# Query projections by seven block products for 18 cross heads, in a fused four-layer kernel on one Trainium2 core

## The chip, the core and the metric

The kernel runs on one core of a Trainium2 chip. The metric is the device time of one execution in microseconds (us). The profile is one execution taken by the hardware profiler. Engines are named PE (TensorE), DVE (VectorE), ACT (ScalarE), POOL (GpSimd) and SP (SyncE, which issues the loads here).

## The reference, cut to what matters

Four layers run one after the other on a stream x of 8 x 128 tokens of width 256, all against the same context of 8 x 128 tokens. Layers 0 and 1 are attention layers with 16 heads of size 16 and an MLP each; layer 3 has a self-attention, a cross-attention and an MLP. Layer 2, in which the change lies, has two cross-attentions with 16 heads of size 128, then an MLP:

```python
def _cross_attention(q_in, kv_in, wq, bq, wk, bk, wv, bv, wo, bo, bias_k, bias_v):
    qh = (q_in @ wq + bq).reshape(b, q_len, H, K)
    kh = (kv_in @ wk + bk).reshape(b, t, H, K)
    vh = (kv_in @ wv + bv).reshape(b, t, H, K)
    kh = jnp.concatenate([kh, jnp.broadcast_to(bias_k, (b, 1, H, K))], axis=1)
    vh = jnp.concatenate([vh, jnp.broadcast_to(bias_v, (b, 1, H, K))], axis=1)
    scale = jnp.sqrt(jnp.asarray(K, q_in.dtype))
    logits = jnp.einsum('bqhk,bthk->bhqt', qh, kh) / scale
    weights = jax.nn.softmax(logits, axis=-1)
    ctx = jnp.einsum('bhqt,bthk->bqhk', weights, vh).reshape(b, q_len, H * K)
    return ctx @ wo + bo
```

H is 16, K is 128. q_in is the normalised stream, kv_in the context.

## The kernel before, in words

All tensors are float32. A product that needs accuracy is made in three passes: each operand is cut into an upper part (rounded to fp32r, "hi") and a lower part (the rest, "lo"), and PE makes hi x hi, hi x lo and lo x hi (`PASSES`). POOL cuts the weights: a cast writes hi, a subtraction writes lo.

**Stages.** Layers 0 and 1 run first and layer 2's MLP and layer 3 last, each by an order written out by hand for every engine (`ORDER_ONE`, `ORDER_TWO`). Between them stand the two cross-attentions of layer 2. They run in 16 turns (`TURNS`): attention j = 1, 2 and turn = 0 to 7, two heads a turn. Below, (j,turn) is a turn. Every engine has its own program, a loop over the turns at the end of `tensor_program`, `vector_program`, `scalar_program` and `gpsimd_program`; each executes its instructions in order, and semaphores tie them together. SP issues the loads in the loop of `sync_program`.

**PE in a turn (L1014 on):** scores of both heads (L960); output projections of the turn before (L994, four pieces); keys of the next turn (L928 or L914); values (L946, four pieces); transposes of the softmax weights (L970); queries of the next turn (L914); weighing of the values (L981). Results go to the eight banks of PSUM. `claim` makes PE wait until the bank's last content has been drained. The keys of the next turn take the banks in which the scores of this turn stand, so they wait for DVE's `bshifted` (L1301); the queries of the next turn take the banks of the values.

**Seven products.** For the keys of (1,3) to (1,7) and (2,1) to (2,7) the 256 x 256 weights of two heads are taken as a matrix of 2 x 2 blocks and the context as 2 x 2 blocks, and their product is made with seven block products instead of eight (`SEVEN`, `seven_products` L920): 21 matmuls of 512 columns instead of 24. POOL makes the sums of the weight blocks, the forms S1 to S4, and cuts them (`cut_forms` L1860, eight operations). The sums of context blocks, the halves T1 to T4, are made once: `begin_halves` on POOL in (1,0) (L1886, six operations), `make_halves` on DVE in (1,1) (L1332, four operations in a chain), upper parts by ACT at the end of (1,1) (L1691), `lower_halves` on POOL after that (L1896, four operations). ACT copies the first product out of its bank (`copy_product` L1633), and DVE adds the others onto it in seven operations (`add_products` L1304, `end_products` L1320). Three of the products take a bank a second time: the fifth waits for ACT's copy, the sixth for DVE's first sum (L1310), the seventh for its second (L1313).

**DVE in a turn (L1423 on):** maximum and shift of both heads' scores (L1296, L1301); output additions (L1379); sum and reciprocal (L1347, L1351); between them the key sums; value drains (L1360); query drains with scale and bias (`queries_of` L1281, which the profile shows as L1072, two per turn); lower parts of the weighed values (L1367).

**ACT in a turn (L1671 on):** exponentials (L1644, L1647); key drains or the product's copy (L1635); copies of the transposed weights (L1655); upper parts of the weighed values (L1485).

**POOL in a turn (L1964 on):** query weights of the next turn (L1846, L1848), value weights of this turn, then the two divides (L1929), each of which waits for DVE's reciprocal; then the keys' forms of the turn after next, the output weights, and in some turns weights of later layers: `cut_up` (L1739, L1741) for M2 and L3c in (2,1) to (2,4), `cut_weights` (L1724, L1726) from (2,5) on. At the end of (1,7) POOL also adds the output bias to x (L2002, four operations).

**Loads.** The weights of the last stage are loaded into `weights` in four pieces in (1,1) to (1,4) (`EARLY`) and three pieces after the last key products (`LATE`), whose places hold the forms and halves until then.

Of the kernel before, what the change touches and what calls it, by code (L numbers as in the profile page):

```python
# [8 lines left out]
F32R = mybir.dt.float32r  # L9
# [43 lines left out]
EARLY = [(0, AT_C["L2_w_fc2"]), (AT_C["L3_w_qkv"], AT_C["L3_w_q"]), (AT_C["L3_w_q"], AT_C["L3_w_co"]), (AT_C["L3_w1"], AT_C["L3_w2"])]  # L53
# [43 lines left out]
def in_seven(j, turn):  # L97

    return turn > 0 and (j, turn) >= (1, 3)
# [6 lines left out]
SEVEN = (("A11", "B11", 0, "product_copied", "P1"), ("S2", "T2", 1, "products_added", "U2"), ("S3", "T3", 2, "products_added", "U3"),  # L106
         ("S1", "T1", 3, "products_added", "C22"), ("A22", "T4", 0, "products_added", "C21"), ("S4", "B22", 1, "products_added", "C12"),
         ("A12", "B21", 2, "products_added", "C11"))
# [41 lines left out]
class Signal:  # L150
# [16 lines left out]
    "w_c_loaded", "w_fc2_loaded", "w_late_loaded", "masks_loaded", "bv_loaded", "wq_loaded0", "wq_loaded1", "wk_loaded0", "wk_loaded1", "wv_loaded", "wo_loaded",  # L167
# [10 lines left out]
    "product_made", "product_copied", "products_added", "form_made", "forms_hi", "forms_lo", "half_made", "half_ended", "halves_hi", "halves_lo",  # L178
# [76 lines left out]
class Memory:  # L255
    def block(self, name, part):
        if name in RAW_BLOCKS:
            return self.k_cut[part][:, RAW_BLOCKS[name], :]
        return self.forms[part][:, MADE_BLOCKS[name], :]

    def half_of(self, name, part):
        if name in HALVES:
            c, n = HALVES[name]
            return self.bcT[part][:, c, n * BANK:(n + 1) * BANK]
        return self.halves[part][:, MADE_HALVES[name], :]

    def __init__(self, nc, ctx):
# [80 lines left out]
        with ExitStack() as b:  # L348
# [7 lines left out]
            self.cut = {n: parts(n, [P, 2, HK]) for n in ("q0", "q1")}  # L356
            self.k_cut = parts("k", [P, 4, HK])
            for n in range(2):
                self.cut[f"k{n}"] = [part[:, 2 * n:2 * n + 2, :] for part in self.k_cut]
# [9 lines left out]
            s2("room", [P, 5600])  # L369
            forms_hi = s2("forms hi", [P, 4, HK], F32R)  # L370
        of_halves, of_forms = (slice(*at) for at in (LATE[1], LATE[2]))
# [293 lines left out]
def tensor_program(nc, m, s, d):  # L665
# [60 lines left out]
    def once(signal, value):  # L726

        if signal not in loaded:
            loaded.add(signal)
            pe.wait_ge(s[signal].sem, value)  # L730
# [1462 lines left out]
```

## Time and profile before

| what | us |
|---|---|
| median of 3 runs | 1036.88 (1036.3 to 1036.94) |
| the profiled execution, its own time | 1035.47 |
| its span, first to last instruction | 1034.2 |
| PE busy | 1000.6 (97%) |
| DVE busy | 767.9 (74%) |
| POOL busy | 651.7 (63%) |
| ACT busy | 577.0 (56%) |

The granted clock of PE is 1.0 of full speed over the whole span. Matmuls overlap, so the time between the starts of two phases says what a phase costs PE, and the durations of single matmuls do not. In a timeline each line has the start, the duration, the engine, the source line, the operation, what it writes and reads, and in brackets the idle time before it with what ended it; a duration after which xN stands covers N instructions.

### The profile page before, as it was taken

What the parts mean: (1) busy time and instruction counts of PE and PEld (TensorE: products, weight loads), DVE (VectorE), ACT (ScalarE), POOL (GpSimd) and SP (SyncE); (2) the same over time, 40 slices, a digit from 0 to 9 for tenths busy, and PEclk for the clock granted to TensorE, in tenths of its full rate; (3) what the DMA queues carried; (4) which work ended last, traced back from release to release, by engine and by line L of the source; (5) the groups of instructions that cost most, each with busy time, mean ns of one, the idle gap of its engine ahead of it and who ended that gap; (6) DMA issues with size and microseconds to landing.
All of it is one profiled execution on the core that took longest, in us unless ns stands there. A gap on an engine that the chain in (4) does not pass through costs nothing.

```text
span 1034.2 us, 21141 instructions
## 1 busy us (share of the span) xinstructions
PE 1000.6 (97%) x8239; PEld 900.8 (87%) x8239; DVE 767.9 (74%) x1229; ACT 577.0 (56%) x1288; POOL 651.7 (63%) x595
## 2 busy tenths in 40 slices
PE   7899999999999999999998999999998999989998
PEld 7788888888899999999997999999998988777877
DVE  7997888998257677876767867777865387898761
ACT  5998888797534422223233332222226489999982
POOL 6885476755578574434367666755534388999960
PEclk9999999999999999999999999999999999999999
DMA  8200001000121220121120111110120000000000
GB/s 329 119 2 2 1 2 42 2 1 2 47 77 42 72 82 28 56 82 42 41 85 21 42 42 42 34 38 12 31 103 1 1 2 1 2 2 2 12 11 21
DMA packets 33931, 40.73 MB, mean 39 GB/s; under 512 B 2127, under 2 KB 31273, under 8 KB 32297
## 3 DMA queue, kind: packets, MB, share of 16 engines
q1 hardware_dynamic: 33833, 39.38, 11.4%
q8 instruction: 67, 1.10, 0.4%
q14 instruction: 31, 0.25, 0.1%
HBM read 38.32 MB, written 1.05 MB: 38 GB/s over the span
## 4 chain that ended last, share of the span: by engine, by line
PE 81%; POOL 9%; DVE 4%; ACT 4%; issue 1%; DMA 0%; SPq 0%; DVEq 0%; ACTq 0%; POOLq 0%
PE psum L914 11%; PE psum L793 9%; PE psum L809 9%; PE psum L946 8%; PE psum L994 8%; PE psum L981 6%; PE psum L928 5%; PE psum L960 5%; PE psum L835 5%; POOL C tile L1792 3%; PE psum L720 3%; PE psum L970 3%; PE psum L825 3%; PE psum L850 2%; POOL C tile L1798 2%; PE psum L864 1%
## 5 line engine op out<-in xcount | busy, mean ns | idle before, releaser
L1929 POOL TENSOR_TENSOR B tile<-B tile,B rec 128x1024 f32<-128x1024 f32 x32 | 61.0, 1909 | 161.6 <-DVE B rec L1351 161.6
L1798 POOL TENSOR_TENSOR A tile<-A tile,outer rec 128x1024 f32<-128x1024 f32 x48 | 91.0, 1905 | 57.9 <-DVE outer rec L1190 57.8
L1655 ACT COPY B PT<-psum 128x512 f32<-128x512 f32 x64 | 32.9, 601 | 139.0 <-PE psum L970 139.0
L1072 DVE TENSOR_SCALAR B qT<-psum,cols 128x1024 f32<-128x1024 f32 (+1 forms) x38 | 44.0, 1166 | 71.6 <-PE psum L914 70.2
L1570 ACT ACTIVATE A tile<-A tile,outer min 128x128 f32<-128x128 f32 (+1 forms) x256 | 92.2, 448 | 2.6 <-DVE outer min L1183 2.5
L1570 ACT ACTIVATE C tile<-C tile,outer min 128x128 f32<-128x128 f32 x256 | 77.9, 399 | 0.5 <-DVE outer min L1183 0.4
L946 PE MATMUL psum<-B v hi,cT hi 128*128 128x256 f32 x256 | 72.1, 282 | 0.3 <-ACT B kT L1485 0.3
L946 PE MATMUL psum<-B v hi,cT lo 128*128 128x256 f32 x256 | 71.8, 281 | 0.0
L946 PE MATMUL psum<-B v lo,cT hi 128*128 128x256 f32 x256 | 71.8, 281 | 0.0
L1798 POOL TENSOR_TENSOR C tile<-C tile,outer rec 128x1024 f32<-128x1024 f32 x32 | 60.5, 1895 | 6.0 <-DVE outer rec L1190 6.0
L1176 DVE TENSOR_TENSOR A tile<-m,psum 128x1024 f32<-128x1024 f32 x48 | 56.5, 1216 | 9.2 <-PE psum L825 8.0
L1188 DVE TENSOR_REDUCE outer sum<-A tile 128x4 f32<-128x1024 f32 (+1 forms) x48 | 58.0, 1208 | 4.9 <-ACT A tile L1570 4.9
L1536 ACT COPY A PT<-psum 128x512 f32<-128x512 f32 x96 | 51.4, 591 | 18.3 <-PE psum L835 10.9
L1485 ACT ACTIVATE B OT0 hi<-psum,cols 128x512 fp32r<-128x512 f32 x32 | 21.9, 688 | 70.9 <-PE psum L981 70.8
L981 PEld LDWEIGHTS psum<-B PT,B v 128*128 128x128 f32 x512 | 59.4, 192 | 1.0
L960 PE MATMUL psum<-B kT,B qT 128*128 128x128 f32 x512 | 59.8, 275 | 0.0
L981 PE MATMUL psum<-B PT,B v 128*128 128x128 f32 x512 | 59.7, 275 | 0.0
L960 PEld LDWEIGHTS psum<-B kT,B qT 128*128 128x128 f32 x512 | 58.5, 192 | 0.1
L809 PE MATMUL psum<-weights,C aT 128*128 128x256 f32 x256 | 57.2, 380 | 1.2 <-ACT C aT L1527 1.2
L809 PE MATMUL psum<-weights,A aT 128*128 128x256 f32 x256 | 57.8, 380 | 0.1
L835 PEld LDWEIGHTS psum<-ident,A tile 128*128 128x128 f32 x384 | 42.1, 141 | 18.2 <-issue 11.4
L1183 DVE TENSOR_REDUCE outer min<-A tile 128x4 f32<-128x1024 f32 (+1 forms) x48 | 55.9, 1207 | 0.0
(327 smaller groups left out, 3470.5 us busy)
## 6 DMA issues: line engine op xcount, KB each, us to landing
weights<-in_weights_c SPq DMA_DIRECT2D x5, 1024.0 KB, 6.3
raw<-in_wq SPq DMA_DIRECT2D x32, 128.0 KB, 2.7
raw<-in_wk SPq DMA_DIRECT2D x32, 128.0 KB, 3.0
raw<-in_wv SPq DMA_DIRECT2D x16, 256.0 KB, 2.8
raw<-in_wo SPq DMA_DIRECT2D x16, 256.0 KB, 2.7
weights<-in_weights_a SPq DMA_DIRECT2D x1, 3072.0 KB, 21.6
weights<-in_weights_a SPq DMA_DIRECT2D x1, 2048.0 KB, 12.4
wide<-in_bias_v SPq DMA_DIRECT2D x2, 1024.0 KB, 10.3
```

The costliest lines, as they stand in the source:

```text
L793: i = pe.matmul(bank(z)[:, n * T:(n + 1) * T], w[wp][:, c, n * P:(n + 1) * P], h[hp][:, c, :], start=(c, wp, hp) == (0, 0, 0), stop=c == C ...
L809: i = pe.matmul(bank(z)[:, 0:D], part.aT(k)[:, c, b * P:(b + 1) * P], w2[:, c, :], start=c == 0, stop=c == FC - 1)
L835: i = pe.transpose(bank(4 + half)[:, j * P:(j + 1) * P], part.tiles[u % 4][:, q * P:(q + 1) * P], m.ident[:, :])
L914: i = pe.matmul(bank(z + n), wt[wp][:, c, :], src[sp][:, c, n * BANK:(n + 1) * BANK], start=(c, wp, sp) == (0, 0, 0), stop=c == C - 1 and ...
L946: i = pe.matmul(bank(z)[:, k * 2 * HK:(k + 1) * 2 * HK], m.bcT[cp][:, c, (2 * n + k) * S:(2 * n + k + 1) * S], m.cut["v"][wp][:, c, :], st ...
L960: i = pe.matmul(bank(z + b // 4)[:, (b % 4) * S:(b % 4 + 1) * S], m.qT[h][:, b * S:(b + 1) * S], m.kT[h][:, b * S:(b + 1) * S], start=True ...
L981: i = pe.matmul(bank(z)[:, k * P:(k + 1) * P], m.vv[:, 4 * n + k, h * HK:(h + 1) * HK], m.bPT[:, h, n, k * P:(k + 1) * P], start=True, sto ...
L994: i = pe.matmul(bank(z)[:, k * D:(k + 1) * D], m.bOT[h][op][:, (2 * n + k) * S:(2 * n + k + 1) * S], m.cut["o"][wp][:, h, :], start=(h, op ...
L1188: dve.tensor_reduce(part.sum[:, u % 4, 0:ly.per], tile(u, ly.nk), AX.X, ALU.add).then_inc(s["sum_made"].sem, s["sum_made"].mark((st, u)))
L1570: i = act.activation(of_head, of_head, ACT.Exp, bias=part.min[:, u % 4, h:h + 1], scale=-1.0)
L1798: pool.tensor_tensor(tile(u, ly.nk), tile(u, ly.nk), part.rec[:, u % 4, 0:ly.per].unsqueeze(2).to_broadcast([P, ly.per, ly.nk]), ALU.mult) ...
L1929: pool.tensor_tensor(tv, tv, m.brec[:, h, :].unsqueeze(2).to_broadcast([P, B, S]), ALU.mult).then_inc(s["normalised"].sem, s["normalised"] ...
```

## The change

- The queries of 18 heads, those of (1,4) to (1,7) and (2,3) to (2,7), come from seven block products too, with their own semaphores, blocks, forms and halves. DVE adds them after the value drains, ACT copies the first after the transposed weights, POOL makes the forms in place of the plain cut. The query and key functions become one, with a `kind`.
- The queries' halves are sums of blocks of the stream and are made for each attention: for j = 1 DVE begins them at the end of (1,1) and ends them at the end of (1,2), ACT makes the upper parts and POOL the lower ones at the end of (1,2); for j = 2 POOL begins them at the end of (2,0), DVE ends them at the end of (2,1), ACT makes the upper parts there, and POOL the lower ones in (2,2), after the divides and before the key forms.
- `make_halves` becomes `end_halves` and moves on DVE from the middle of (1,1) to its end, behind `weigh_heads`.
- In (2,0) ACT copies the first key product between the two exponentials, not after them.
- POOL adds the output bias in (2,0), after the output weights' cut, not at the end of (1,7).
- The four cuts of L3c's up-weights move on POOL from (2,1) to (2,4) to the end of (2,7). Their weights, L3's first output weights and L3c's query weights (1.5 MB in three pieces) are loaded after the last query products.
- The factor 1/sqrt(128) moves from the query drain and two column scalings to the exponential.

```diff
-EARLY = [(0, AT_C["L2_w_fc2"]), (AT_C["L3_w_qkv"], AT_C["L3_w_q"]), (AT_C["L3_w_q"], AT_C["L3_w_co"]), (AT_C["L3_w1"], AT_C["L3_w2"])]
+LATER = [(AT_C["L3_w1"], AT_C["L3_w2"]), (AT_C["L3_w_ao"], AT_C["L3_w_q"]), (AT_C["L3_w_q"], AT_C["L3_w_kv"])]
+EARLY = [(0, AT_C["L2_w_fc2"]), (AT_C["L3_w_qkv"], AT_C["L3_w_ao"]), (AT_C["L3_w_kv"], AT_C["L3_w_co"])]
...
-def in_seven(j, turn):
-
-    return turn > 0 and (j, turn) >= (1, 3)
+FIRST_SEVEN = {("k", 1): 3, ("k", 2): 1, ("q", 1): 4, ("q", 2): 3}
+
+
+def in_seven(kind, j, turn):
+
+    return turn >= FIRST_SEVEN[kind, j]
...
     def project_pair(j, kind, turn):
-        if kind == "k" and in_seven(j, turn):
-            seven_products(j, turn)
+        if in_seven(kind, j, turn):
+            seven_products(j, kind, turn)
             return
...
-        affine(m.qT[head % 2][:, :], m.psum[:, z:z + 2, :].rearrange("p a b -> p (a b)"), SCALEK, m.col[f"L2_bq{j}"][:, head:head + 1]).then_inc(
+        affine(m.qT[head % 2][:, :], m.psum[:, z:z + 2, :].rearrange("p a b -> p (a b)"), None, m.col[f"L2_bq{j}"][:, head:head + 1]).then_inc(
...
+    def begin_halves(j, kind):
+        made, raw = s[kind + "_half_begun"], m.halves_raw[kind]
+        for name, of, (less, more), spare in (("T1", 0, ("B11", "B12"), 2), ("T3", 2, ("B12", "B22"), 3)):
+            if name == "T3":
+                dve.wait_ge(made.sem, made.at((j, "T1")))
+            dve.tensor_tensor(raw[:, of, :], m.half_of(kind, more, 0), m.half_of(kind, less, 0), ALU.subtract)
+            dve.tensor_tensor(raw[:, spare, :], m.half_of(kind, more, 1), m.half_of(kind, less, 1), ALU.subtract).then_inc(made.sem, made.mark((j, "lo", name)))
+            dve.wait_ge(made.sem, made.at((j, "lo", name)))
+            dve.tensor_tensor(raw[:, of, :], raw[:, of, :], raw[:, spare, :], ALU.add).then_inc(made.sem, made.mark((j, name)))
...
+        shared = {kind: not last and in_seven(kind, j, turn + 1) for kind in "kq"}
+        if shared["k"]:
+            add_products(j, "k", turn + 1)
         divide_by_sum(j, turn, 1)
-        if shared:
-            end_products(j, turn + 1)
-        if (j, turn) == (1, 1):
-            make_halves()
+        if shared["k"]:
+            end_products(j, "k", turn + 1)
         for n in range(4) if turn else ():
             values_of(j, turn, n)
-        if not last:
+        if shared["q"]:
+            add_products(j, "q", turn + 1)
+            end_products(j, "q", turn + 1)
+        elif not last:
             queries_of(j, 2 * turn + 2)
             queries_of(j, 2 * turn + 3)
         for h in range(2):
             weigh_heads(j, turn, h)
+        if (j, turn) == (1, 1):
+            end_halves(1, "k")
+            begin_halves(1, "q")
+        if (j, turn) in ((1, 2), (2, 1)):
+            end_halves(j, "q")
...
-        for h in range(2):
-            exponentials(j, turn, h)
-        if not last and in_seven(j, turn + 1):
-            copy_product(j, turn + 1)
-        elif not last:
+        exponentials(j, turn, 0)
+        if (j, turn) == (2, 0):
+            copy_product(2, "k", 1)
+        exponentials(j, turn, 1)
+        if turn and not last and in_seven("k", j, turn + 1):
+            copy_product(j, "k", turn + 1)
+        elif not last and not in_seven("k", j, turn + 1):
             keys_of(j, 2 * turn + 2)
             keys_of(j, 2 * turn + 3)
         for h in range(2):
             turn_weights(j, turn, h)
+        if not last and in_seven("q", j, turn + 1):
+            copy_product(j, "q", turn + 1)
...
+        if (j, turn) == (2, 2):
+            lower_halves(2, "q")
         if turn < NP_ - 2:
             cut_pair(j, "k", turn + 2)
         elif (j, turn) == (1, NP_ - 2):
             cut_pair(2, "k", 0)
         cut_output(j, turn)
         if (j, turn) == (1, 0):
-            begin_halves()
+            begin_halves(1, "k")
         if (j, turn) == (1, 1):
-            lower_halves()
+            lower_halves(1, "k")
+        if (j, turn) == (1, 2):
+            lower_halves(1, "q")
+        if (j, turn) == (2, 0):
+            bias_x()
+            begin_halves(2, "q")
         if (j, turn) == (1, NP_ - 1):
             cut_pair(2, "q", 0)
         if j == 2 and 1 <= turn < 5:
             cut_up("M2", turn - 1)
-            cut_up("L3c", turn - 1)
...
+        if (j, turn) == (2, NP_ - 1):
+            for n in range(4):
+                cut_up("L3c", n)
...
+    sp.wait_ge(s["q_product_made"].sem, s["q_product_made"].at((2, NP_ - 1, "A12")))
+    for at in LATER:
+        load_last("w_later_loaded", *at)
```

## Rows read from the trace of the kernel before

**Rows 1.** The page: busy time, the chain that ended last, one costly group
```profile
PE 1000.6 (97%) x8239; PEld 900.8 (87%) x8239; DVE 767.9 (74%) x1229; ACT 577.0 (56%) x1288; POOL 651.7 (63%) x595
...
PE 81%; POOL 9%; DVE 4%; ACT 4%; issue 1%; DMA 0%; SPq 0%; DVEq 0%; ACTq 0%; POOLq 0%
...
L1929 POOL TENSOR_TENSOR B tile<-B tile,B rec 128x1024 f32<-128x1024 f32 x32 | 61.0, 1909 | 161.6 <-DVE B rec L1351 161.6
```

**Rows 2.** Timeline of PE in (1,2): keys, sixth product, values, queries, weighing
```profile
365.50 0.40 PE L928 MATMUL psum<-cT hi,B k hi 128*128 128x512 f32 x1
...
368.95 0.40 PE L928 MATMUL psum<-cT hi,B forms hi 128*128 128x512 f32 x1
...
370.32 0.28 PE L946 MATMUL psum<-B v hi,cT hi 128*128 128x256 f32 x1
...
377.64 0.47 PE L914 MATMUL psum<-B hT hi,B q1 hi 128*128 128x512 f32 x1
...
383.21 3.73 PE L981 MATMUL psum<-B PT,B v 128*128 128x128 f32 x32
```

**Rows 3.** Timeline of DVE from the end of (1,1) through (1,2)
```profile
356.20 1.65 DVE L1367 SCALAR_TENSOR_TENSOR B OT1 lo<-psum,cols,B OT1 hi 128x512 fp32r<-128x512 f32 x2
358.17 1.22 DVE L1296 TENSOR_REDUCE B max<-psum 128x8 f32<-128x1024 f32 x1 [0.32 <-PE psum L960]
...
367.16 0.69 DVE L1310 TENSOR_TENSOR B kT<-psum,B kT 128x512 f32<-128x512 f32 x1 [0.40 <-PE psum L928]
...
380.69 1.28 DVE L1072 TENSOR_SCALAR B qT<-psum,cols 128x1024 f32<-128x1024 f32 x1 [3.82 <-PE psum L914]
```

**Rows 4.** Timeline of POOL: divide and key forms in (1,2); one cut in (2,1)
```profile
371.55 1.90 POOL L1929 TENSOR_TENSOR B tile<-B tile,B rec 128x1024 f32<-128x1024 f32 x1 [2.76 <-DVE B rec L1351]
373.41 0.46 POOL L1870 TENSOR_TENSOR weights<-raw 128x128 f32<-128x128 f32 x1
...
378.42 0.61 POOL L1846 CAST B o hi<-raw 128x512 fp32r<-128x512 f32 x1
...
603.33 0.61 POOL L1739 CAST C w1 hi<-weights 128x512 fp32r<-128x512 f32 x1
...
605.25 0.39 POOL L1846 CAST B q1 hi<-raw 128x256 fp32r<-128x256 f32 x1
```

**Rows 5.** Timelines of DVE, POOL and PE in (2,0) and (2,1)
```profile
564.06 0.69 DVE L1310 TENSOR_TENSOR B kT<-psum,B kT 128x512 f32<-128x512 f32 x1 [0.56 <-ACT B kT L1635]
...
575.98 1.29 POOL L1848 TENSOR_TENSOR B o lo<-raw,B o hi 128x512 fp32r<-128x512 f32 x1
...
591.36 0.28 PE L946 MATMUL psum<-B v hi,cT hi 128*128 128x256 f32 x1
```

**Rows 6.** Timelines of DVE and POOL in (1,1): halves, and POOL's work beside
```profile
336.77 0.64 DVE L1335 TENSOR_TENSOR weights<-cT hi,weights 128x512 f32<-128x512 f32 x1
337.45 2.27 DVE L1337 TENSOR_TENSOR weights<-weights,cT lo 128x512 f32<-128x512 f32 x1
...
336.94 2.23 POOL L1929 TENSOR_TENSOR B tile<-B tile,B rec 128x1024 f32<-128x1024 f32 x1 [0.64 <-DVE B rec L1351]
...
357.65 5.01 POOL L1899 TENSOR_TENSOR weights lo<-weights,weights lo 128x512 fp32r<-128x512 f32 x4 [9.91 <-ACT weights lo L1691]
```

**Rows 7.** Timeline of POOL at the end of (1,0): begun halves, then cuts
```profile
321.43 1.27 POOL L1891 TENSOR_TENSOR weights<-cT hi 128x512 f32<-128x512 f32 x1
...
329.17 0.40 POOL L1846 CAST B q1 hi<-raw 128x256 fp32r<-128x256 f32 x1
...
331.49 0.61 POOL L1846 CAST B v hi<-raw 128x512 fp32r<-128x512 f32 x1
```

**Rows 8.** Timeline of POOL at the end of (2,7), and a DMA group
```profile
777.31 1.29 POOL L1726 TENSOR_TENSOR weights lo<-weights,C qkv hi 128x512 fp32r<-128x512 f32 x1
778.54 1.93 POOL L2006 MEMSET C vaug<- 128x512 f32 x4
788.05 0.70 POOL L1713 TENSOR_TENSOR outer rstd<-outer ve,half 128x2 f32<-128x2 f32 x1 [7.59 <-DVE outer ve L1113]
...
weights<-in_weights_c SPq DMA_DIRECT2D x5, 1024.0 KB, 6.3
```

More of the change, by code:

```diff
@@ L355, in __init__ @@
             self.kT = [s2(f"kT{k}", [P, B * S]) for k in range(2)]
[L356 to L359, printed above, removed]
+            self.cut, self.blocks = {}, {}
+            for kind in "qk":
+                self.blocks[kind] = parts(kind, [P, 4, HK])
+                for n in range(2):
+                    self.cut[f"{kind}{n}"] = [part[:, 2 * n:2 * n + 2, :] for part in self.blocks[kind]]
             self.cut["v"] = parts("v", [P, 2, 2 * HK])
@@ L1688, in scalar_program @@
         if (j, turn) == (1, 1):
-            act.wait_ge(s["half_ended"].sem, s["half_ended"].at("T4"))
-            for n in range(4):
-                act.copy(m.halves[0][:, n, :], m.halves_raw[:, n, :]).then_inc(s["halves_hi"].sem, s["halves_hi"].mark(n))
+            upper_halves(1, "k")
+        if (j, turn) in ((1, 2), (2, 1)):
+            upper_halves(j, "q")
         if last and j == 1:
@@ L1858, in cut_head, with bias_x, cut_forms @@
         cut(j, f"{kind}{k}", head, (f"w{kind}_loaded{k}", 16 * ((j - 1) * NP_ + head // 2 + 1)))
-    def cut_forms(j, turn):
-        made, raw, forms, event = s["form_made"], m.k_raw, m.forms_raw, (j, turn)
+    def bias_x():
+        for k in range(NS):
+            pool.wait_ge(s["nxn_made"].sem, s["nxn_made"].at((k, SB - 1)))
+            pool.tensor_tensor(m.x(k), m.x(k), m.row("L2_bo2").unsqueeze(1).to_broadcast([P, SB, D]), ALU.add).then_inc(
+                s["x_biased"].sem, s["x_biased"].mark(k))
+    def cut_forms(j, kind, turn):
+        made, upper, lower = s[kind + "_form_made"], s[kind + "_forms_hi"], s[kind + "_forms_lo"]
+        raw, forms, blocks, event = m.blocks_raw[kind], m.forms_raw[kind], m.blocks[kind], (j, turn)
         a21, a22, a11, a12 = (raw[:, n, :] for n in range(4))
@@ L1888, in begin_halves @@
+        pool.tensor_tensor(m.forms[kind][1][:, :, :], forms[:, :, :], m.forms[kind][0][:, :, :], ALU.subtract).then_inc(
+            lower.sem, lower.mark((*event, "made")))
+    def begin_halves(j, kind):
+        made, raw = s[kind + "_half_made"], m.halves_raw[kind]
         for name, of, (less, more), spare in (("T1", 0, ("B11", "B12"), 2), ("T3", 2, ("B12", "B22"), 3)):
             if name == "T3":
-                pool.wait_ge(made.sem, made.at("T1"))
-            pool.tensor_tensor(raw[:, of, :], m.half_of(more, 0), m.half_of(less, 0), ALU.subtract)
@@ L1892, in begin_halves @@
[L1892 to L1896 removed]
+                pool.wait_ge(made.sem, made.at((j, "T1")))
+            pool.tensor_tensor(raw[:, of, :], m.half_of(kind, more, 0), m.half_of(kind, less, 0), ALU.subtract)
@@ L1897, in lower_halves @@
+            pool.tensor_tensor(raw[:, spare, :], m.half_of(kind, more, 1), m.half_of(kind, less, 1), ALU.subtract).then_inc(made.sem, made.mark((j, "lo", name)))
+            pool.wait_ge(made.sem, made.at((j, "lo", name)))
+            pool.tensor_tensor(raw[:, of, :], raw[:, of, :], raw[:, spare, :], ALU.add).then_inc(made.sem, made.mark((j, name)))
+    def lower_halves(j, kind):
+        hi, lo = s[kind + "_halves_hi"], s[kind + "_halves_lo"]
         for n in range(4):
-            pool.wait_ge(s["halves_hi"].sem, s["halves_hi"].at(n))
@@ L1991, in gpsimd_program @@
             cut_weights("L3c", "kv"[turn - 5])
+        if (j, turn) == (2, NP_ - 1):
+            for n in range(4):
+                cut_up("L3c", n)
         if last and j == 1:
```

190 lines of the change are left out of this document (96 added, 94 removed).

## The prediction

> **What bounds the kernel now.** I read the page first, then the timeline of each engine over one turn. The page [rows 1] has TensorE (PE) busy for 97% of the span and carrying 81% of the chain that ended last. GpSimd (POOL) idles 161.6 us ahead of its 32 divides, 5 us each. So the idle time of the others is worth nothing by itself; what counts is where PE waits for them.
>
> In turn (1,2) (attention 1, turn 2; I write (j,turn) throughout) PE starts the key products at 365.50, the values at 370.32, the queries at 377.64 and the weighing at 383.21 [rows 2], one behind the other. VectorE (DVE) has room in the second half of a turn, 3.82 us ahead of the first query drain, and almost none in the first: from the maximum at 358.17 to the first key sum at 367.16 it waits 0.40 us [rows 3]. These slacks can be read off, and the change spends them in a few places.
>
> **Query products.** Plain queries take PE 383.21 - 377.64 = 5.57 us a turn (24 matmuls), seven products 370.32 - 365.50 = 4.82 us (21) [rows 2]. Nine turns take the new form, (1,4) to (1,7) and (2,3) to (2,7): 9 x 0.75 = **6.7 us** gained.
>
> For each of them DVE makes seven sums of some 0.7 us in place of two drains of 1.28 us [rows 3]. The last should end, as in the keys, within 2 us of the last product. PE weighs for 3.73 us [rows 2] before the scores want it, and DVE's own next work starts about then. I cost the sums at nothing; their cover is DVE's idle 3.82 us, and ACT (ScalarE) makes its copy when it waits for the weighing. Without cover each turn gives back its 0.75.
>
> POOL's cut of the queries grows from four operations, 2.3 us, to the eight of the keys, 378.42 - 373.41 = 5.0 us [rows 4]. The 2.7 more lie ahead of a divide, where POOL idles; nothing is due there.
>
> **The key copy, turn (2,0).** DVE's first key sum waits 0.56 us for ACT's copy [rows 5]. With the copy ahead of the second exponential that wait goes, and DVE, busy until then, is the next that is late. The bias additions leave the place before the forms, so PE has those earlier, but its sixth product wants the same sum. Gain: **0.6 us** for both edits.
>
> **DVE at the end of (1,1): ten subtractions before the next maximum.** Before, DVE made the key halves in mid-turn, where it had room. Now four operations that end the key halves and six that begin the query halves stand between the last output part, which ends at 356.20 + 1.65 = 357.85, and the maximum at 358.17 [rows 3]. A start follows the last by 0.7 us [rows 6]. Four end at 360.7, ten at 364.9: a lag of 6.7 us.
>
> They also meet POOL. The second of the four took 2.27 us beside a POOL multiplication that took 2.23 [rows 6] where it takes 1.90 alone [rows 4]. Now POOL makes its four lower halves, 5.01 us, 1.25 each [rows 6], from about 361.5, while DVE is at its fifth to tenth. I let them take turns, which adds 4 x 1.25 less 0.3 of overlap: DVE ends at 369.6, a lag of 11.4.
>
> The Trainium skill, "SBUF — State Buffer", section "SBUF: two separate sides", says that a DVE operation with two SBUF inputs and a GpSimd one that reads SBUF lock each other out for the whole instruction. The trace agrees where it shows the case (2.27 us beside 2.23); by this rule the sum is the one below, without it that of the first rival.
>
> What PE feels: its key products claim the score banks and wait for DVE. The first sum ended at 367.16 + 0.69 = 367.85 after waiting 0.40 for PE [rows 3]; the product that takes its bank starts at 368.95 [rows 2]. So 1.5 us of lag are free. PE loses 11.4 - 1.5 = **9.9 us** in (1,2), 5.2 if nothing meets at the port. Outputs aside, everything behind on PE's queue is later by the same.
>
> **End of (1,2), felt in (1,3).** Four subtractions, 2.8 us, of which DVE had 0.3 idle, with POOL waiting for them: lag 2.5, loss 1.0. Then POOL has the four lower halves (5.0, from 0.65 us after DVE's maximum starts), the new query cut 5.0 and the value cut 1.9 (the same two operations as in 605.25 - 603.33 [rows 4]), and ends 12.5 us after that maximum. PE wants the values 370.32 - 358.17 = 12.15 us after an undelayed one [rows 2, 3], here 12.15 - 2.5 + 1.0 = 10.65. It waits 1.9. Together **2.9 us**.
>
> **POOL at the end of (2,0), felt in (2,1).** The output cut ends at 577.3 [rows 5], less the 0.6 gained. Then come four bias additions of 1.25, the six begun halves in 329.17 - 321.43 = 7.7, the query cuts in 331.49 - 329.17 = 2.3 [rows 7] and the value cut, 1.9: 576.7 + 16.9 = 593.6. PE wants the values at 591.36 [rows 5], now 590.8. It waits **2.8 us**. The DMA wait that now stands before the query cut vanishes in this.
>
> **End of (2,1), felt in (2,2).** Four subtractions, lag 2.5 alone. POOL, late from the step before, is in its query forms and value cut, so I add 2.5 for blocked starts: lag 5.0, loss 3.5 (1.0 at the low end). Next, the lower halves stand after the divides: the second divide ends 371.55 + 1.90 - 358.17 = 15.3 us after the maximum [rows 3, 4], and 5.0 more is 20.3. The query products would start 19.5 us after an undelayed maximum [rows 2, 3], 18.0 after this one. PE waits 2.3. Together **5.8 us**.
>
> **The tail.** The four cuts of the last up-weights leave (2,1) to (2,4), where POOL idled, for the end of (2,7): 4 x 1.92 = 7.7 us after 777.31 + 1.29 = 778.6, then 1.9 of memsets, ending at 788.2. The first root of the last stage ran at 788.05 after an idle 7.59 [rows 8]: **0.2 us**. Three loads (1.5 MB) are issued later, after the last query products, most of a turn before POOL wants them; 1 MB lands in 6.3 us [rows 8], and on SP's queue only two other late loads stand behind. Two tiny scalings go near the start: nothing.
>
> **The sum.** Lost: 9.9 + 2.9 + 2.8 + 5.8 + 0.2 = 21.6. Gained: 6.7 + 0.6 = 7.3. Net +14.3 us. The profiled execution took 1035.47 us (span 1034.2, 1.3 outside it), 1.4 under the median of 1036.88. Against its own time the sum gives 1049.8; against the median, which is what will be measured, **1051.2**. A measurement of this kernel can tell about 0.2% (2.1 us) from no change.
>
> **Rivals.**
> - *No clash at the port.* DVE ends its ten at 364.9 and PE loses 5.2 there, 3.3 in (2,2). Net 5.2 + 2.9 + 2.8 + 3.3 + 0.2 - 7.3 = +7.1: 1044.0. For it: one overlap in the trace is thin evidence, and DVE's many operations on PSUM run beside POOL unharmed. Against: [rows 6] is the very operation. Chance 0.15.
> - *The lags never reach PE.* The place is the key products of (1,2). If the slack there and before the value cuts is larger than I read, only the saving is left: 1036.9 - 7.3 = 1029.6, faster. It decides when all losses together stay under 7.3, which (1,2) alone exceeds unless it costs a fraction of my figure. For it: POOL's idle time is large on the whole. Against: PE's queue runs in order and its claims are written out. Chance 0.10; another 0.03 that losses and gains cancel, at about 1037.
> - *The query products give nothing.* DVE's sums or POOL's forms hold PE up in each of the nine turns: 1051.2 + 6.7 = 1057.9. Against: the keys do the same without it. Chance 0.07.
>
> **How the numbers follow.** The forecast has 0.65, with its own range 1047 to 1055: 9.9 and 5.8 can each be 2 too much, and blocked starts can add 3. For 8 in 10 the range reaches down past the first rival to 1041. Faster 0.10, same 0.03, slower 0.87.
>
> **What would show it.** In the changed kernel's trace: query products of 4.8 us in nine turns; the maximum of (1,2) some 11 us after the last output part, with DVE subtractions of 1.3 to 2 us in between; PE idle for several us in and before the key products of (1,2); waits of PE for POOL's value cut in (1,3) and (2,1), and for the lower halves before the queries of (2,2). I am wrong if PE has under 7 us of waits between (1,1) and (2,3), or if those ten subtractions take 0.7 us each.

## The result, and the profile after

The changed kernel takes **1050.99 us**, median of 4 runs (1049.48 to 1052.34), against 1036.59 for the kernel before beside it (4 runs, 1035.2 to 1036.94): a ratio of 1.0142, with a 95% interval of 1.0129 to 1.0155. It is 14 us slower; 1051.2 was forecast. The profiled execution took 1049.48 us, its span 1048.3.

The page of the kernel after, to be read against [rows 1]:

```profile
PE 1004.6 (96%) x8212; PEld 900.8 (86%) x8212; DVE 799.6 (76%) x1286; ACT 586.3 (56%) x1305; POOL 697.4 (67%) x645
...
PEclk9999999999999989999999999999999999999999
...
PE 71%; POOL 13%; DVE 8%; ACT 4%; issue 3%; DMA 0%; SPq 0%; DVEq 0%; POOLq 0%; ACTq 0%
...
L1983 POOL TENSOR_TENSOR B tile<-B tile,B rec 128x1024 f32<-128x1024 f32 x32 | 60.7, 1900 | 116.5 <-DVE B rec L1379 116.5
```

PE's share of the chain fell from 81% to 71%; POOL and DVE took it. POOL's idle time ahead of the divides fell from 161.6 to 116.5 us, as it has 45.7 us more work. One slice of the granted clock shows 8, where before there was none. 27 matmul instructions fewer (three in each of nine turns) say that the query products are there.

What PE waited for in the attentions, longest first (the view of waits, PE, 300 to 800 us of the kernel after; columns: engine, what the instruction writes and its line, the releaser; us in total, times, longest):

```profile
PE psum L946 <- DVE B tile L1319: 5.5, 1, 5.5
PE psum L946 <- DVE B kT L1328: 4.4, 4, 1.7
PE psum L964 <- POOL B v lo L1895: 3.1, 2, 1.9
PE psum L946 <- POOL weights lo L1953: 1.8, 1, 1.8
```

Before, the longest single wait in this stretch was one of 1.5 us, for ACT's copy in (2,0), and none of these four rows was there. The first row is the key products of (1,2) waiting for DVE's shift, the second the sixth key product waiting for DVE's first sum, in (1,2), (1,3), (2,0) and (2,2), the third the values of (1,3) and (2,1) waiting for POOL's value cut, the last the queries of (2,2) waiting for the lower halves.

DVE at the end of (1,1), which answers to [rows 3] (timeline of the kernel after):

```profile
357.17 0.68 DVE L1363 TENSOR_TENSOR weights<-cT hi,weights 128x512 f32<-128x512 f32 x1
...
360.55 0.69 DVE L1356 TENSOR_TENSOR weights<-B hT lo 128x512 f32<-128x512 f32 x1
361.27 1.67 DVE L1358 TENSOR_TENSOR weights<-weights 128x512 f32<-128x512 f32 x1
362.98 1.67 DVE L1355 TENSOR_TENSOR weights<-B hT hi 128x512 f32<-128x512 f32 x1
364.57 1.76 DVE L1356 TENSOR_TENSOR weights<-B hT lo 128x512 f32<-128x512 f32 x1
366.36 1.63 DVE L1358 TENSOR_TENSOR weights<-weights 128x512 f32<-128x512 f32 x1
367.92 1.21 DVE L1314 TENSOR_REDUCE B max<-psum 128x8 f32<-128x1024 f32 x1
```

And POOL and PE behind it (timelines, the same kernel):

```profile
360.77 6.68 POOL L1953 TENSOR_TENSOR weights lo<-weights,weights lo 128x512 fp32r<-128x512 f32 x4 [14.30 <-ACT weights lo L1676]
...
370.53 0.77 PE L946 MATMUL psum<-cT hi,B k hi 128*128 128x512 f32 x1 [5.47 <-DVE B tile L1319]
371.10 0.63 PE L946 MATMUL psum<-cT lo,B k hi 128*128 128x512 f32 x1
...
377.16 0.50 PE L946 MATMUL psum<-cT hi,B k forms hi 128*128 128x512 f32 x1 [0.30 <-DVE B kT L1328]
...
378.75 0.28 PE L964 MATMUL psum<-B v hi,cT hi 128*128 128x256 f32 x1
```

Ten operations stand between the output parts and the maximum. Six take 0.68 to 0.69 us. The last four take 1.63 to 1.76, and they are the ones beside POOL's four lower halves, which take 6.68 us together against the 5.01 of [rows 6]. The maximum is 10.35 us later than its normal place (357.57, 1.97 behind the start of the last output part, as in [rows 3]); this delay of DVE's maximum is called the lag below. PE reaches the key products and stops for 5.47 us.

The same comparison for whole turns, from the start of one turn's scores to the next (read off PE's timeline). "Plain" is the length with no wait:

| turn | before | after | what is in it |
|---|---|---|---|
| (1,2) | 30.60 | 39.41 | + 8.8, DVE's lag |
| (1,3) | 30.60 | 32.98 | - 0.6 query products, + 0.8 keys, + 2.2 value cut |
| (1,4) to (1,6), (2,3) to (2,6) | 30.60 | 29.99 | - 0.61 each |
| (2,0) | 21.96 | 22.85 | - 0.7 for the copy, + 1.6 low clock |
| (2,1) | 30.60 | 31.93 | + 1.3, value cut |
| (2,2) | 30.60 | 34.46 | - 0.6, + 2.7 keys, + 1.8 lower halves |

The gains are 9 x 0.61 = 5.5 and 0.7; the losses 8.8, 3.0 and, over (2,0) to (2,2), 1.6 + 1.3 + 4.5 = 7.4. That is 13.0 more at the end of the attentions. The stage began 0.6 us earlier in this execution (324.29 against 324.89; in other kernels of this study it began anywhere from 324.3 to 327.4), and 1.6 came later, nearly all of it behind 900 us. 13.0 - 0.6 + 1.6 = 14.0, the difference of the two executions (1049.48 - 1035.47).

Two of these items were in no step of the prediction: a lower clock in (2,0), and one behind 900 us. The granted clock by stretches of the kernel after (windows of PE: stretch; its length, busy time and instructions; granted clock; DMA share; GB/s):

```profile
360.00:365.00 5.00, 5.00 (x43) 1.00 0.00 0
365.00:370.00 5.00, 0.06 (x1) 0.94 0.00 0
370.00:376.00 6.00, 5.47 (x13) 0.50 0.16 48
376.00:380.00 4.00, 3.69 (x20) 0.97 0.00 0
572.00:574.00 2.00, 1.13 (x4) 1.00 0.00 0
574.00:578.00 4.00, 4.00 (x12) 0.57 0.00 0
578.00:580.00 2.00, 2.00 (x11) 1.00 0.00 0
```

In (1,2) that is hidden, since DVE is late with its first key sum anyway (377.16 waits 0.30 for it): in e5_plain below the same stretch is half as long, 370.17 to 373.59, PE then waits 1.57 us for that sum, and (1,2) is 39.41 us all the same. In (2,0) nothing hides it.

### The profile page after: what moved, and what is told of

It reads as the page before. It is cut to its first block, busy times and chain, and to the rows that moved or that the text cites. A ratio compares the mean times of both kernels' runs of the same rounds, so it can differ in the third digit from the quotient of the medians.

```text
span 1048.3 us, 21233 instructions
## 1 busy us (share of the span) xinstructions
PE 1004.6 (96%) x8212; PEld 900.8 (86%) x8212; DVE 799.6 (76%) x1286; ACT 586.3 (56%) x1305; POOL 697.4 (67%) x645
## 4 chain that ended last, share of the span: by engine, by line
PE 71%; POOL 13%; DVE 8%; ACT 4%; issue 3%; DMA 0%; SPq 0%; DVEq 0%; POOLq 0%; ACTq 0%
PE psum L810 9%; PE psum L826 9%; PE psum L946 8%; PE psum L964 7%; PE psum L931 5%; PE psum L1012 5%; PE psum L852 5%; PE psum L999 5%; PE psum L978 4%; PE psum L738 3%; PE psum L842 3%; PE psum L867 3%; POOL C tile L1839 2%; PE psum L988 2%; PE psum L881 2%
## 5 line engine op out<-in xcount | busy, mean ns | idle before, releaser
L1983 POOL TENSOR_TENSOR B tile<-B tile,B rec 128x1024 f32<-128x1024 f32 x32 | 60.7, 1900 | 116.5 <-DVE B rec L1379 116.5
L852 PEld LDWEIGHTS psum<-ident,A tile 128*128 128x128 f32 x384 | 42.1, 141 | 18.2 <-issue 11.4
L1388 DVE TENSOR_TENSOR B v<-psum,B bv 128x512 f32<-128x512 f32 x64 | 42.1, 684 | 18.4 <-PE psum L964 17.5
```

Of the source, the lines that this page charges most:

```text
L852: i = pe.transpose(bank(4 + half)[:, j * P:(j + 1) * P], part.tiles[u % 4][:, q * P:(q + 1) * P], m.ident[:, :])
L1983: pool.tensor_tensor(tv, tv, m.brec[:, h, :].unsqueeze(2).to_broadcast([P, B, S]), ALU.mult).then_inc(s["normalised"].sem, s["normalised"] ...
```

## The experiments

The theory at this point: the loss is waits of PE at five places, each caused by what the change puts on DVE or POOL ahead of something PE wants, and the query products themselves gain. The rivals: DVE's ten operations are not what counts, but POOL's lower halves; the long DVE operations come from something other than POOL; the query products gain nothing. Below, "changed" is the changed kernel.

**e1_order.** In (1,1) the halves of the queries first:

```diff
         if (j, turn) == (1, 1):
-            end_halves(1, "k")
             begin_halves(1, "q")
+            end_halves(1, "k")
```

> The changed kernel with one swap on DVE at the end of (1,1): the six operations that begin the query halves come before the four that end the key halves, so POOL, which waits for the latter, is idle during all ten. Theory (a port that DVE and POOL lock against each other): all ten take 0.7 us, the maximum of (1,2) starts 7 us after the last output part instead of 10.7, and PE's key products are now held by POOL's lower key halves, which end some 13 us after it; PE's loss in (1,2) falls from 9.0 to 5 to 7 us, the time to 1047 to 1049. Rival (the operations are slow by themselves, because of their operands): four of them still take 1.6 to 1.8 us and the time stays at 1051.

Measured: 1049.44 us, ratio 1.0147 [1.0119, 1.0175], no different from the changed kernel. DVE and then POOL and PE (timelines of e1_order):

```profile
357.94 0.68 DVE L1355 TENSOR_TENSOR weights<-B hT hi 128x512 f32<-128x512 f32 x1
...
364.09 0.69 DVE L1369 TENSOR_TENSOR weights<-weights,cT lo 128x512 f32<-128x512 f32 x1
364.70 1.21 DVE L1314 TENSOR_REDUCE B max<-psum 128x8 f32<-128x1024 f32 x1
```

```profile
365.51 4.95 POOL L1953 TENSOR_TENSOR weights lo<-weights,weights lo 128x512 fp32r<-128x512 f32 x4 [18.29 <-ACT weights lo L1676]
...
370.72 0.77 PE L946 MATMUL psum<-cT hi,B k hi 128*128 128x512 f32 x1 [4.89 <-POOL weights lo L1953]
```

With POOL's lower halves behind them, all ten operations take 0.7 us and DVE's lag is 6.4 instead of 10.35. PE still starts its keys at 370.72, because now it waits for the lower halves. So the clash is real, and undoing it alone saves only what the next late thing leaves: (1,2) fell from 39.41 to 36.91, 2.5 us. It was lost again further on: (1,3) is 34.64 instead of 32.98, where the granted clock is low from 411.3 to 414.7, and (2,0) and (2,1) together are 56.43 instead of 54.79, where the low stretch stands behind the wait for the value cut (602.4 to 605.9) and no longer in (2,0).

**e2_ten_mid.** The ten operations where DVE has room, in mid-turn:

```diff
+        if (j, turn) == (1, 1):
+            end_halves(1, "k")
         for n in range(4) if turn else ():
             values_of(j, turn, n)
+        if (j, turn) == (1, 1):
+            begin_halves(1, "q")
...
-        if (j, turn) == (1, 1):
-            end_halves(1, "k")
-            begin_halves(1, "q")
```

> The changed kernel with all ten halves operations of (1,1) in mid-turn: the four ahead of the value drains, as before the change, the six behind them. Theory (DVE's lag ahead of the maximum is what PE feels in (1,2)): the maximum of (1,2) is on time, PE starts the key products without a wait, the 9.0 us lost there go, 1042. Rival (half of that loss is PE's lowered clock or POOL's lower halves): 1044 to 1047.

Measured: 1043.04 us, ratio 1.0078 [1.0053, 1.0104], 8.0 under the changed kernel by the medians; by the two ratios, each to the kernel before timed beside it, 6.6. In the traces (1,2) is 30.60 us, to the hundredth what it was before, 8.8 less than in the changed kernel; the other turns of the table keep their losses and are 1.1 longer together ((1,3) 33.19, (2,1) 32.14, (2,2) 35.14, with a low clock from 626.9 to 630.3). In mid-turn two of the ten are held up as well, and it costs nothing (timeline of e2_ten_mid):

```profile
336.84 2.27 DVE L1365 TENSOR_TENSOR weights<-weights,cT lo 128x512 f32<-128x512 f32 x1
...
346.24 1.78 DVE L1356 TENSOR_TENSOR weights<-B hT lo 128x512 f32<-128x512 f32 x1
...
357.56 1.23 DVE L1314 TENSOR_REDUCE B max<-psum 128x8 f32<-128x1024 f32 x1 [0.32 <-PE psum L978]
```

The maximum has its 0.32 us of idle back, as in [rows 3]. The place of the ten operations is the whole loss of (1,2), 8.8 us.

**e3_ends_mid.** The four operations that end the query halves, in (1,2) and (2,1), likewise ahead of the query drains:

```diff
+        if (j, turn) in ((1, 2), (2, 1)):
+            end_halves(j, "q")
         if shared["q"]:
             add_products(j, "q", turn + 1)
             end_products(j, "q", turn + 1)
...
-        if (j, turn) in ((1, 2), (2, 1)):
-            end_halves(j, "q")
```

> The changed kernel with the four operations that end the query halves ahead of the query drains in (1,2) and (2,1) rather than behind the output parts. Theory: the key products of (1,3) and (2,2) are on time (2.6 to 3.6 us back), POOL gets the upper halves 3 us earlier, so most of the wait for the value cut in (1,3) goes and the wait for the lower halves in (2,2) shrinks from 2.0 to about 1: some 6 us less, 1045. Rival (POOL's own work sets these two turns, not DVE's lag): 2 us less or nothing, 1049 to 1051.

Measured: 1043.11 us, ratio 1.0077 [1.006, 1.0093]. (1,3) is 29.98, so both of its waits are gone, that for DVE's sum and that for the value cut. The prediction priced the two apart, yet one place of four operations makes both. POOL shows why (timelines, first of the changed kernel, then of e3_ends_mid):

```profile
400.16 5.06 POOL L1953 TENSOR_TENSOR weights lo<-weights,B q halves hi 128x512 fp32r<-128x512 f32 x4 [10.50 <-ACT B q halves hi L1676]
```

```profile
397.03 5.02 POOL L1953 TENSOR_TENSOR weights lo<-weights,B q halves hi 128x512 fp32r<-128x512 f32 x4 [5.25 <-ACT B q halves hi L1676]
```

POOL had been idle for 10.5 us, waiting for ACT, and ACT for DVE's four operations. Made earlier, they let POOL begin 3.7 us sooner (1.5 us behind the start of the scores of (1,3), at 395.56, in place of 5.2 behind it, at 394.99), and its value cut is in time. (2,2) is 31.01: what is left above 29.99 is 1.0 of lower halves (PE waits 0.78 for them there). (2,0) fell from 22.85 to 21.23, since the clock stayed at 1.00 there, and (2,1) rose from 31.93 to 35.20: PE, that much earlier, waits 2.9 us for the value cut and then has its low clock there, 601.5 to 604.9.

**e4_bias_back.** The bias additions again at the end of (1,7):

```diff
         if (j, turn) == (2, 0):
-            bias_x()
             begin_halves(2, "q")
...
                     lower_part(2, k, m.nh[k])
+            bias_x()
```

> The changed kernel with the bias additions back at the end of (1,7). Theory: POOL reaches the value cut of (2,1) 5 us earlier, so PE's 1.5 us wait there goes, and POOL is no longer in the way of DVE's four operations at the end of (2,1), so the loss at the keys of (2,2) falls from 2.6 to 1.0; in (2,0) the forms are late again by 0.5. Some 2.5 us less, 1048.5. Rival (the additions' new place is a gain, as it frees the forms): 1 us more, 1052.

Measured: 1049.09 us, ratio 1.0132 [1.0116, 1.0147]: 1.9 less than the changed kernel, less than the runs of one kernel differ (1049.48 to 1052.34). Yet (2,1) is 30.60, without a wait. The gain went elsewhere: (1,3) is 34.62 and (2,2) 35.41, each with a stretch of low clock that the changed kernel does not have there (414.9 to 418.3 and 636.8 to 640.2). The other half of the expectation failed too: DVE's four operations at the end of (2,1) were not freed. They take 0.92, 1.64, 0.98 and 1.68 us, more than in the changed kernel. What sets POOL's query forms and value cut beside them is not lateness from (2,0): ahead of the forms POOL waits for the load of the query weights in both kernels, 2.42 us to 617.41 in the changed one, 2.39 us to 617.80 here. (2,0) is 21.23 with the additions ahead of the forms, as short as anywhere; moving them out of the way had no use.

**e5_plain.** No query products at all; everything else as changed. A second edit, not shown, lets the loads of the last pieces wait for the plain queries:

```diff
-FIRST_SEVEN = {("k", 1): 3, ("k", 2): 1, ("q", 1): 4, ("q", 2): 3}
+FIRST_SEVEN = {("k", 1): 3, ("k", 2): 1, ("q", 1): 8, ("q", 2): 8}
```

> The changed kernel with plain query products in all turns; halves, moves and loads stay, and the last loads wait for the last plain queries. It shows what the nine turns of seven products are worth. Theory: PE takes 5.5 us in place of 4.95 for the queries in nine turns (5.5 us more), but POOL's query cut is 2.7 us shorter, so the wait for the value cut in (1,3) goes (1.9), and nothing waits for the lower query halves in (2,2) (2.0): 1.5 us more on the whole, 1052.5. Rival (the query products give nothing, the turns are bound elsewhere): 4 us less, 1047.

Measured: 1050.92 us, ratio 1.0143 [1.013, 1.0156], the same as the changed kernel. The turns that had query products are 30.60 again (one of them, (2,4), 30.39), which is 0.61 a turn or 5.5 us in nine. But two turns are free of most of what the changed kernel loses there:

- (1,3) is 31.44, only 0.84 above plain: with POOL's plain cut of 2.3 us in place of 5.0 the value cut is in time.
- (2,2) is 31.45, 0.85 above plain: nobody waits for lower halves, and the keys lose 0.85 instead of 2.7. POOL, with less to cut, is through before DVE's four operations at the end of (2,1) (timelines of the changed kernel, then of e5_plain):

```profile
621.12 0.98 DVE L1365 TENSOR_TENSOR weights<-weights,B hT lo 128x512 f32<-128x512 f32 x1
622.13 1.66 DVE L1367 TENSOR_TENSOR weights<-B hT hi,weights 128x512 f32<-128x512 f32 x1
```

```profile
622.80 0.69 DVE L1365 TENSOR_TENSOR weights<-weights,B hT lo 128x512 f32<-128x512 f32 x1
623.53 0.69 DVE L1367 TENSOR_TENSOR weights<-B hT hi,weights 128x512 f32<-128x512 f32 x1
```

So the products' gain of 5.5 is real, and it is spent on waits that they alone cause in this placement: 2.2 us in (1,3) and 3.6 in (2,2), of which 1.8 are the lower halves and 1.8 the keys. Against that, (2,0) and (2,1) together are 1.3 us longer in e5_plain, as its low clock stands behind the longer wait in (2,1). From the scores of (1,1) to the last scores the changed kernel takes 448.94 us and this one 449.75, which leaves 0.8 of the 5.5.

**e6_all.** The edits of e2, e3 and e4 together, which are not shown again, and in (2,2) the lower halves ahead of the divides:

```diff
         if turn:
             cut_values(j, turn)
+        if (j, turn) == (2, 2):
+            lower_halves(2, "q")
         for h in range(2):
             divide(j, turn, h)
-        if (j, turn) == (2, 2):
-            lower_halves(2, "q")
```

> The changed kernel with all halves operations of DVE in mid-turn, the bias additions back at the end of (1,7), and POOL's lower query halves of attention 2 ahead of the divides of (2,2). Theory (the changed kernel's loss is late queues in four places, its products' saving is real): PE waits nowhere for long in the turns, 5.5 us under the kernel before, 1031. Rival (the extra work of DVE and POOL must show somewhere, since the whole is bound by more than PE): 1035 to 1040.

Measured: **1030.4 us**, ratio 0.9939 [0.9926, 0.9951]. It is faster than both kernels: 5.3 us under the kernel before in the same comparison (1035.68), and 20.6 under the changed one. Every turn from (1,3) to (2,6) is 29.98 or 29.99, but for the last of attention 1, (2,0) at 21.22 and (2,1) at 30.60 (its queries are plain). What PE waits for from 300 to 800 us (view of waits, e6_all):

```profile
PE psum L717 <- ACT C xn L1520: 1.6, 2, 1.4
...
PE psum L946 <- DVE B kT L1328: 0.9, 1, 0.9
```

The waits of 5.5, 3.1 and 1.8 us are gone, and with them each low clock between 300 and 800 us. From the scores of (1,1) to the last scores this kernel takes 429.69 us and the kernel before 435.93: 6.2 less, which is the 5.5 of the query products and the 0.7 of the copy. Some 1.8 of that is lost again behind the last scores, where this profile has a low clock twice (892.9 to 896.3 and 913.3 to 916.8) and that of the kernel before has none.

**e7_copy_only.** The kernel before, with nothing but ACT's copy in (2,0) moved between the exponentials:

```diff
-        for h in range(2):
-            exponentials(j, turn, h)
-        if not last and in_seven(j, turn + 1):
+        exponentials(j, turn, 0)
+        if (j, turn) == (2, 0):
+            copy_product(2, 1)
+        exponentials(j, turn, 1)
+        if turn and not last and in_seven(j, turn + 1):
```

> The kernel before with one edit of the change: ACT copies the first key product of (2,0) between the two exponentials. Theory (DVE's first sum is next late): 0.5 us less, 1036.1, which the trace shows and the times hardly. Rival (ACT's copy was the only thing late): PE's 1.5 us wait goes, 1035.

Measured: 1036.09 us, ratio 1.0002 [0.9992, 1.0012]. In the trace (2,0) is 21.27 instead of 21.96, so the 0.7 us is there; in the whole time it can't be told from nothing.

**e8_six_end.** The four key operations in mid-turn, the six query ones at the end of (1,1). This is to meet the clash again with the old place of the lower halves:

```diff
+        if (j, turn) == (1, 1):
+            end_halves(1, "k")
         for n in range(4) if turn else ():
             values_of(j, turn, n)
...
         if (j, turn) == (1, 1):
-            end_halves(1, "k")
             begin_halves(1, "q")
```

> The changed kernel with the four operations that end the key halves back ahead of the value drains of (1,1); only the six that begin the query halves stay at its end. ACT then has the upper halves early and POOL makes its four lower halves from about 357.1, as before the change, beside those six. Port clash: the six take turns with POOL, a lag of 6 x 0.7 + 4 x 1.0 = 8.2 us (1.0 is what a blocked operation took more in the changed kernel, 1.63 to 1.76 instead of 0.69), less 1.5 free: (1,2) is 6.7 us longer than its 30.60, and the median is some 2.1 us under the changed kernel, 1048.9. Rival, no clash (the long operations of the changed kernel had another cause): the six take 0.7 each, the lag is 4.2, (1,2) is 2.7 longer, and the median is about 1044.9.

Measured: 1049.28 us, ratio 1.0123 [1.0095, 1.015]; (1,2) is 37.94, 7.3 above plain where 6.7 was expected with the clash and 2.7 without. The lag itself is 8.3 (the maximum is at 366.21, 10.24 behind the start of the last output part in place of 1.97), where 8.2 was expected. DVE and POOL (timelines of e8_six_end):

```profile
357.53 1.71 DVE L1355 TENSOR_TENSOR weights<-B hT hi 128x512 f32<-128x512 f32 x1
359.17 1.77 DVE L1356 TENSOR_TENSOR weights<-B hT lo 128x512 f32<-128x512 f32 x1
360.96 1.67 DVE L1358 TENSOR_TENSOR weights<-weights 128x512 f32<-128x512 f32 x1
362.67 1.67 DVE L1355 TENSOR_TENSOR weights<-B hT hi 128x512 f32<-128x512 f32 x1
364.26 0.88 DVE L1356 TENSOR_TENSOR weights<-B hT lo 128x512 f32<-128x512 f32 x1
```

```profile
357.42 6.37 POOL L1954 TENSOR_TENSOR weights lo<-weights,weights lo 128x512 fp32r<-128x512 f32 x4 [9.90 <-ACT weights lo L1677]
```

In the changed kernel the first of these operations, at 359.95, took 0.68 us. With POOL's four now beside it, it takes 1.71, as do the next three, and POOL's 6.37 fit four turns. That the long operations follow POOL's work, wherever it is put, is the evidence for the clash: early in e8_six_end, late in the changed kernel, nowhere in e1_order.

**e9_idle.** The kernel of e6_all, with idle time for PE made on purpose in turns where it has none:

```diff
+        for i in range({(1, 4): 4, (2, 3): 2, (2, 5): 8}.get((j, turn), 0) if h == 0 else 0):
+            dve.tensor_reduce(mx, sc, AX.X, ALU.max).then_inc(s["max_made"].sem, s["max_made"].mark((*event, i)))
+            dve.wait_ge(s["max_made"].sem, s["max_made"].at((*event, i)))
         dve.tensor_reduce(mx, sc, AX.X, ALU.max).then_inc(s["max_made"].sem, s["max_made"].mark(event))
```

> The version with all repairs (1030.4 us), with repeated maxima ahead of the first maximum on DVE: four in (1,4), two in (2,3), eight in (2,5), where nothing else holds PE up. A repeat takes 1.25 us. The lags are 5.0, 2.5 and 10.0, less 1.5 free each: PE waits 3.5, 1.0 and 8.5 us, and the time is 13.0 us more, 1043.4. Theory, the long wait itself is what lowers the clock: the granted clock shows stretches at 0.50 after the waits of 3.5 and 8.5 and none after that of 1.0; they cost from nothing (where DVE is still behind) to 1.6 us each, so 1043.4 to 1046.6. Rival, the low stretches belong to something else in the changed kernel: the clock stays at 1.00 in all three turns, and the time is 1043.4.

Measured: 1046.24 us, one run. The turns are 35.12 for (1,4), 31.03 for (2,3) and 38.57 for (2,5), or 5.1, 1.0 and 8.6 above 29.99; the lags alone were to give 3.5, 1.0 and 8.5. That is 14.75 us. The stage began 2.7 us later than in e6_all, ahead of anything that the edit touches, and what lies behind the last scores is 2.1 us shorter, as this profile has no low clock there; together 15.4, the difference of the two executions. The longest single waits of PE in these turns are 1.74, 0.81 and 5.19 us and not 3.5, 1.0 and 8.5: a lag comes out as several waits, in (1,4) of 0.16 and 0.66 for DVE's shifts and 1.74 for its first sum. The clock around the key products of (1,4), and of (2,5) (windows of PE, e9_idle):

```profile
433.00:436.00 3.00, 1.26 (x5) 1.00 0.00 0
436.00:438.00 2.00, 2.00 (x9) 0.70 0.02 4
438.00:440.00 2.00, 2.00 (x11) 0.50 0.00 0
440.00:442.00 2.00, 2.00 (x18) 0.95 0.00 0
```

```profile
714.00:716.00 2.00, 0.00 (x0) 1.00 0.00 0
716.00:718.00 2.00, 0.00 (x0) 0.67 0.00 0
718.00:720.00 2.00, 1.99 (x5) 0.50 0.00 0
```

In (2,3), where the added wait is small, the clock stays at 1.00. In e6_all these turns have no low clock and no wait, and nothing but the repeats was added, so waiting is enough to bring the lower level. This rests on one profile of each kernel. In (1,4) it costs the 1.6 us that the turn has beyond its lag, because the slow matmuls are those of the values, which nothing covers. In (2,5) it costs 0.1, because they are the key products, which outrun DVE's sums anyway. The same two cases are (2,0) and (1,2) of the changed kernel.

## Why the prediction was right, and where its terms were off

**The mechanism and the places were right: PE's queue waits for DVE and POOL in (1,2), (1,3), (2,1) and (2,2), as listed. That the time, 1051.2 forecast and 1050.99 measured, is met to 0.2 us is luck; the terms are not that close.** Point by point:

- *Ten operations ahead of the maximum, 9.9 us.* Measured 8.8, all of it from this cause (e2_ten_mid). The lag was 10.35 and not 11.4, for taking turns added 6.73 - 4 x 0.69 = 4.0 us and not 4.7, and the ten alone are 6.4 (e1_order) and not 6.7. The clash at the port was real, four operations of 1.63 to 1.76 us; the Trainium skill, "SBUF — State Buffer", section "SBUF: two separate sides", had it right, and this case shows it three times over. The free 1.5 us of lag held: 10.35 - 1.5 = 8.85.
- *(1,3), 2.9.* Measured 3.0, 0.84 of it from DVE (e5_plain has it alone) and 2.2 the value cut, where 1.0 and 1.9 were forecast.
- *POOL at the end of (2,0), 2.8.* In the changed kernel (2,1) shows 1.3. The step was right: where (2,0) has no low clock ahead of it the value matmuls wait 2.88 us (e1_order) or 2.86 (e5_plain). The low clock in (2,0) made PE 1.6 us late, and so its wait shorter by as much. Two delays of PE that lie ahead of the same late POOL don't add.
- *(2,2), 5.8.* Measured 4.5: 1.8 for the lower halves against 2.3, and 2.7 for the keys against 3.5. The lag was 3.9 where 5.0 was put in: DVE's four were held up as foreseen, but three of them and not all, and two of those by little (0.98, 1.66 and 0.98 us). POOL was there at that time, but not because it was late from the step before, as the prediction has it: it waits 2.42 us for a load ahead of its query forms (e4_bias_back), and the forms are 2.7 us longer than the plain cut. With POOL done in time the lag is 2.4 and the loss 0.85 (e5_plain), close to the 2.5 and 1.0 of the prediction's low end.
- *Query products, 9 x 0.75 = 6.7.* Measured 9 x 0.61 = 5.5. The mis-sized term is the price of the seven products, taken from the keys' 4.82 us. From the first query product to the weighing it is 4.94 (449.44 to 454.38 in (1,4)), while the keys of the same turn take 4.83 (437.29 to 442.12).
- *The copy and the bias additions, 0.6.* Measured 0.7, and all of it is the copy's (e7_copy_only). What that step says of the bias additions, that the earlier forms give nothing since the sixth product wants the same sum, held (e4_bias_back).
- *The tail, 0.2.* PE shows no loss at the stage's start: the distance between the two kernels is 12.4 us there and still 12.5 at 856 us of the kernel before.
- *Not in the sum: TensorE's clock.* It costs 1.6 us in (2,0), less what (2,1) then waits less, and some 1.6 us came behind 900 us, where its profile has two low stretches.

So the losses in the attentions were forecast at 21.4 and came to 19.2, the gains at 7.3 and came to 6.2: a net of 13.0 instead of 14.1, and the low clock behind 900 us made up the rest. Terms that were somewhat too large on both sides and a cost that was not foreseen met in the right place. The rival without the clash (1044.0) falls by the timelines of the changed kernel and of e8_six_end. The rival that the lags never reach PE falls by the 5.47 us wait. The rival that the query products give nothing (1057.9) named the wrong place: DVE and POOL do keep up in seven of the nine turns. But its conclusion was nearer than it looked: as e5_plain shows, the products earn 5.5 us and give 4.7 back on the whole, through (1,3) and (2,2).

What stays open is the low clock behind 900 us. The changed kernel and e5_plain have it from 912 and from 933, e6_all from 893 and from 913 (the same two places, as its last scores are 19 us earlier), e2_ten_mid at 1002, e8_six_end at 1012; the kernel before, e1_order, e3_ends_mid, e4_bias_back, e7_copy_only and e9_idle do not. Ahead of the first of these places PE waits 1.01 and 0.80 us in the changed kernel, at 1.00 until then, and 1.01 and 0.81 in the kernel before, where no fall follows. So the waits alone don't explain it; there is one profile of each kernel, and no run was made for it.

## What to carry to other kernels

Work that is needed only a turn later goes where the engine has idle time in its turn, not where the code of the turn ends: on an engine that runs in order, the end of a loop's body stands right ahead of the next turn's first result. The same 18 operations of DVE cost 8.8 us and more in one place and nothing in another. When operations are moved, look at what the other engine of a shared port does at the new place, and take a saving only after the waits that it causes itself have been taken off: here they ate 4.7 of 5.5 us, beside the 15 us that the rest of the change costs by e5_plain. With four pieces of code in other places 20.6 us came back.

## What the runs showed of the hardware that was not expected

- After waits of PE the granted clock falls to its lower level for a few microseconds: during the 5.47 us without a matmul in (1,2) of the changed kernel, from 574.2 to 577.6 after a wait of 1.67, and in e9_idle during one of 5.19 (0.67 between 716 and 718, while PE still stood still) and after one of 1.74 with others close ahead. The kernel before and e7_copy_only show 1.00 throughout, with waits of up to 1.5 us. A stretch costs 1.6 us where PE sets the pace and next to nothing where PE's products outrun what drains them.
- It does not follow each such wait. (1,3) waits 1.86 us for the value cut in the changed kernel at 1.00, while the same turn of e1_order, after 1.87 us, has a low stretch from 411.3 to 414.7 and takes 34.64 instead of 32.98. In (2,0) the wait of 1.66 us is followed by no fall in e1_order and e3_ends_mid, and by one in e2_ten_mid. Whether this is what spreads the times of a kernel (1041.38 to 1047.32 for e2_ten_mid, 1028.87 to 1030.8 for e6_all) is not shown: e7_copy_only, whose waits are as short as those of e6_all, spreads from 1034.17 to 1039.04.
- Two operations that share the port don't only slow down, they alternate: DVE's take 1.63 to 1.77 us, their own 0.7 plus most of one of POOL's 1.25, and POOL's group of four grows from 5.01 us to 6.68 and 6.37.
